# A state-space layer on one core: bias by matmul, a shorter softplus, a reordered instruction list and a split prologue

## The reference, cut to what matters

```
xz  = in_proj_w @ xn            # 512 rows: x half (256), z half (256)
for each direction (forward, reversed):
    u     = silu(conv4(x) + conv_bias)                     # 256 channels, 4 taps
    x_dbl = xproj_w @ u                                    # 8 rows for delta, 16 B, 16 C
    delta = softplus(dtproj_w @ x_dbl[:8] + dt_bias)
    dA    = exp(delta * A);  dBx = delta * B * u           # 256 channels x 16 states
    h[t]  = dA[t] * h[t-1] + dBx[t]                        # the scan
    y     = (sum over states of h * C + D * u) * silu(z)
branch 1 = out_proj_w @ (y_forward + y_reversed)
branch 2 = ternary(weight) @ quantize4(hadamard(xn))       # per-token scale, round, clip to -8..7
```

## Time and profile before

| | |
|---|---|
| median of three runs | 982.82 us |
| profiled execution | 989.38 us, span 987.6 us |
| TensorE busy | 802.9 us, 81% |
| VectorE busy | 787.0 us, 80% |
| ScalarE busy | 780.7 us, 79% |
| GpSimd busy | 788.1 us, 80% |
| mean granted clock of TensorE | 0.875 of 2.4 GHz |
| DMA, mean over the span | 73 GB/s |

### The profile page before, as it was taken

The page is one execution under the profiler, slowest core; times in us unless marked ns, Lnnn a source line. Parts: engine busy times, 40 slices in busy tenths (PEclk is TensorE's granted clock), DMA queues, the critical chain, the costliest instruction groups (busy, mean ns, idle before and its releaser), DMA issues.

```text
span 987.6 us, 13840 instructions
## 1 busy us (share of the span) xinstructions
PE 802.9 (81%) x3873; PEld 381.5 (39%) x3873; DVE 787.0 (80%) x795; ACT 780.7 (79%) x1452; POOL 788.1 (80%) x493
## 2 busy tenths in 40 slices
PE   2478887979888897888889797897978889797974
PEld 1134434343443434333353434434343343434352
DVE  2248887988888888888789887888978887988982
ACT  2469896988959887798869889698887988699950
POOL 1038978997899887898789977989879897798994
PEclk9677998899998989889879989889898898898796
DMA  3070607051160605215070421607043150704300
GB/s 86 11 162 29 135 4 182 3 123 41 57 136 3 159 3 124 68 53 107 3 170 24 115 44 39 154 3 159 3 104 88 33 129 3 169 15 99 61 22 11
DMA packets 50841, 72.44 MB, mean 73 GB/s; under 512 B 6128, under 2 KB 19328, under 8 KB 50816
## 3 DMA queue, kind: packets, MB, share of 16 engines
q1 hardware_dynamic: 50384, 71.87, 31.3%
q10 hardware_dynamic: 432, 0.26, 0.1%
HBM read 60.58 MB, written 11.53 MB: 73 GB/s over the span
## 4 chain that ended last, share of the span: by engine, by line
POOL 33%; issue 32%; ACT 13%; PE 11%; DVE 7%; SPq 1%; DMA 1%; POOLq 1%; DVEq 0%; ACTq 0%
POOL hst L612 22%; ACT da L370 5%; POOL dbx_t L622 5%; DVE hst L512 4%; PE pb L744 3%; ACT dbx_t L359 3%; POOL t_log L628 3%; PE b_ps L827 2%; PE b_ps L824 2%; POOL xn L674 2%; DVE b_ps L500 1%; PE pb L751 1%; PE y L841 1%; DMA rep<-d_scr 1%; PE pb L771 1%
## 5 line engine op out<-in xcount | busy, mean ns | idle before, releaser
L612 POOL TENSOR_TENSOR hst<-hst,c_rep 128x1024 f32<-128x1024 f32 x256 | 601.4, 2365 | 132.2 <-DVE hst L512 128.4
L512 DVE TENSOR_TENSOR_SCAN hst<-da,b_ps 128x512 f32<-128x512 f32 x512 | 589.5, 1203 | 82.1 <-ACT da L370 43.4
L827 PE MATMUL b_ps<-ident,dbx_t 128*128 128x128 f32 x1536 | 241.9, 298 | 127.3 <-DVE hst L512 120.1
L370 ACT ACTIVATE da<-rep,neg_a 128x511 f32<-128x511 f32 x512 | 335.6, 709 | 6.4 <-DMA rep<-d_scr 6.3
L827 PEld LDWEIGHTS b_ps<-ident,dbx_t 128*128 128x128 f32 x1536 | 178.2, 150 | 277.5 <-DVE hst L512 230.1
L359 ACT ACTIVATE dbx_t<-du_t,b_t 128x256 f32<-128x256 f32 x576 | 248.1, 495 | 2.9 <-PE b_ps L827 2.9
L841 PE MATMUL y<-hst,sum_sel 128*32 128x512 f32 x1024 | 166.6, 730 | 0.0
L744 PE MATMUL pb<-xnt,conv_wt 128*128 128x512 f32 x256 | 120.7, 616 | 0.7 <-ACT xnt L291 0.7
L824 PE MATMUL b_ps<-t_log,spread_sel 32*128 32x512 f32 x256 | 89.3, 698 | 10.6 <-DVE hst L512 10.6
L500 DVE TENSOR_TENSOR b_ps<-b_ps,b_rep 128x1024 f32<-128x1024 f32 x64 | 78.1, 1220 | 21.6 <-PE b_ps L824 21.6
L622 POOL TENSOR_TENSOR dbx_t<-du_t,b_t 128x1024 f32<-128x1024 f32 x48 | 91.2, 1901 | 2.7 <-ACT du_t L342 2.7
(11 more groups left out here) (90 smaller groups left out, 598.5 us busy)
## 6 DMA issues: line engine op xcount, KB each, us to landing
rep<-d_scr SPq DMA_DIRECT2D x128, 256.0 KB, 9.3
c_rep<-bc_scr SPq DMA_DIRECT2D x64, 256.0 KB, 5.0
d_scr<-t_pos SPq DMA_DIRECT2D x16, 512.0 KB, 3.0
b_rep<-bc_scr SPq DMA_DIRECT2D x64, 64.0 KB, 2.4
x_ln<-x SPq DMA_DIRECT2D x8, 256.0 KB, 3.2
x_res<-x SPq DMA_DIRECT2D x8, 256.0 KB, 2.9
out<-x_res SPq DMA_DIRECT2D x8, 256.0 KB, 9.5
conv_wt<-conv_w SPq DMA_DIRECT2D x2, 512.0 KB, 5.9
```

The costliest lines, as they stand in the source:

```text
L370: nc.scalar.activation(da[s % 2][:, j, 1:L], rep[d][h][:, j, 1:L], ACT.Exp, scale=neg_a[:, d, h, j, q:q + 1]).then_inc(decay_done, 1)
L512: nc.vector.tensor_tensor_scan(hst[s % RING][:, j, :], da[s % 2][:, j, :], b_ps[:, j, :], 0.0, ALU.mult, ALU.add).then_inc(scan_done, 1)
L612: nc.gpsimd.tensor_tensor(hst[s % RING][:, two, :], hst[s % RING][:, two, :], c_rep[d][:, q:q + 1, :].broadcast_to([P, 2, L]), ALU.mult).t ...
L827: ins = tr(b_ps[:, j, P * c:P * (c + 1)], dbx_t[(NX * d + q - 1) % 2][:, c, NJ * h + j, :, :].rearrange("p r e -> p (r e)"), ident[:, :])
```

## The change

Five things are done together.

Bias by matmul: row 64 of `dtw` holds the convolution's bias, and `conv` ends each half with a fifth matmul, that one row against a broadcast one. `u_sigmoid` is then one tanh pass; `make_u` is (tanh + 1) * `pb`, twice u, and factors of 0.5 and 0.25 go into `xproj` and `skip`. The bias of delta comes in the same way, through a row of `dtw` and a row of ones in `xdbl`.

Softplus: the Relu passes go; 1 + exp is written to `t_pos` in SBUF rather than to `pb`, `log1p` works on `t_pos`, and `delta` takes max(`pb`, 0) itself.

Lists: on ScalarE, VectorE (`times_b` one scan earlier), GpSimd and TensorE (both convolution halves in slot 7 of both units) the order is another one.

Quantizer: clip and rescale are VectorE's, in slot 6, on `pb`.

Prologue: ScalarE waits for the weights later, the two halves of the first unit's softplus, delta, du and replication go separately, and B and C are replicated first.

```diff
@@ TensorE
                 for k in taps:
-                    ins = mm(pb[:, 1 - h, :], conv_wt[d][:, k, P * h:P * (h + 1)], window, start=k == 0, stop=k == TAPS - 1)
+                    mm(pb[:, 1 - h, :], conv_wt[d][:, k, P * h:P * (h + 1)], window, start=k == 0, stop=False)
+                ins = mm(pb[:, 1 - h, :], dtw[d][BIAS:BIAS + 1, P * h:P * (h + 1)], ident[BIAS:BIAS + 1, BIAS:BIAS + 1].broadcast_to([1, L]), start=False, stop=True)
...
                     if s == 7 and not last(b):
                         if d == 0:
-                            conv(d, U + 2, 1, range(TAPS), dut_ready, 2 * V + 2)
-                        else:
-                            conv(d, U + 2, 0, range(TAPS), dut_ready, 2 * V + 1)
+                            pe.wait_ge(xnt_ready, b + 2)
+                        conv(d, U + 2, 0, range(TAPS), dut_ready, 2 * V + 1)
                     next_inputs(s, 1)
...
                     if s == 6 and nxt:
                         if d == 1:
-                            du_transposed(V, 1, had_read, b + 1)
-                        elif not last(b):
-                            pe.wait_ge(xnt_ready, b + 2)
-                            conv(d, U + 2, 0, range(TAPS), dut_ready, 2 * V + 1)
-                    if s == 7 and d == 1 and not last(b):
+                            du_transposed(V, 1, xq_ready, b + 1)
+                    if s == 7 and not last(b):
                         conv(d, U + 2, 1, range(TAPS), dut_ready, 2 * V + 2)
@@ ScalarE
-                nc.scalar.activation(t_exp[:, h, :], pb[:, 1 - h, :], ACT.Tanh, bias=half_bias[:, d, h:h + 1], scale=0.5).then_inc(u_step, 1)
-                act.wait_ge(u_step, 2 * V + h + 1)
-                nc.scalar.activation(t_exp[:, h, :], t_exp[:, h, :], ACT.Copy, bias=0.5, scale=0.5).then_inc(u_sig, 1)
+                nc.scalar.activation(t_exp[:, h, :], pb[:, 1 - h, :], ACT.Tanh, scale=0.5).then_inc(u_sig, 1)
...
-                nc.scalar.activation(xdbl[d][0:XC, :], pb[0:XC, 1, :], ACT.Copy).then_inc(xdbl_ready, 1)
+                nc.scalar.activation(xdbl[d][0:XC, :], pb[0:XC, 1, :], ACT.Identity, bias=ident[0:XC, ONE:ONE + 1]).then_inc(xdbl_ready, 1)
...
             def softplus_in(d, V):
+                for n, h in enumerate((1, 0)):
+                    act.wait_ge(dt_filled, 2 * V + n + 1)
+                    nc.scalar.activation(t_exp[:, h, :], pb[:, h, :], ACT.Abs).then_inc(sp_step, 1)
-                    nc.scalar.activation(t_exp[:, h, :], pb[:, h, :], ACT.Abs, bias=col[:, d, 1, h:h + 1]).then_inc(sp_step, 1)
-                    nc.scalar.activation(t_pos[:, h, :], pb[:, h, :], ACT.Relu, bias=col[:, d, 1, h:h + 1]).then_inc(sp_step, 1)
...
-                nc.scalar.activation(pb[:, :, :], t_exp[:, :, :], ACT.Copy, bias=1.0).then_inc(sp_step, 1)
+                nc.scalar.activation(t_pos[:, :, :], t_exp[:, :, :], ACT.Copy, bias=1.0).then_inc(sp_step, 1)
...
-                nc.scalar.activation(t_log[:, :, :], pb[:, :, :], ACT.Ln).then_inc(log_ready, 1)
+                nc.scalar.activation(t_log[:, :, :], t_pos[:, :, :], ACT.Ln).then_inc(log_ready, 1)
@@ ScalarE's list of a unit, after
+                for s in range(SLOTS):
+                    decays(b, d, s, 0)
+                    if s == 0:
+                        if d == 0 and not first(b):
+                            keep_dut(d, U, 1)
+                        inputs_t(d, U, 1, 1)
+                    if s == 1:
+                        inputs_t(d, U, 1, 3)
+                        if nxt:
+                            u_sigmoid(e, V, 1)
+                    if s == 2:
+                        if nxt:
+                            keep_xdbl(e, V)
+                        if d == 0 and not first(b):
+                            keep_xqt(b - 1)
+                        inputs_t(d, U, 2, 2)
+                    if s == 3 and nxt:
+                        softplus_log(V)
+                        if d == 0 and not last(b):
+                            log_var(b + 1)
+                    if s in (4, 5):
+                        inputs_t(d, U, 3, 2 * (s - 4))
+                    if s == 6 and d == 0 and not last(b):
+                        normalize(b + 1)
+                    if s == 7 and d == 0:
+                        if not last(b):
+                            keep_xnt(b + 1)
+                        keep_dut(e, V, 0)
+                    decays(b, d, s, 1)
+                    if s == 0:
+                        inputs_t(d, U, 1, 2)
+                        if nxt:
+                            u_sigmoid(e, V, 0)
+                    if s == 1:
+                        inputs_t(d, U, 2, 0)
+                        inputs_t(d, U, 2, 1)
+                    if s == 2:
+                        inputs_t(d, U, 2, 3)
+                        if nxt:
+                            keep_bt(e, V)
+                            softplus_in(e, V)
+                    if s == 3 and d == 0 and not last(b):
+                        guess_rstd(b + 1)
+                    if s in (4, 5):
+                        inputs_t(d, U, 3, 2 * (s - 4) + 1)
+                    if s == 5 and d == 0:
+                        z_sigmoid(b)
+                    if s == 6 and d == 0:
+                        keep_longer(b)
+                    if s == 7 and nxt:
+                        keep_dut(e, V, 1 - d)
+                        inputs_t(e, V, 1, 0)
@@ VectorE
-                nc.vector.scalar_tensor_tensor(u[d][:, h, :], pb[:, 1 - h, :], col[:, d, 0, h:h + 1], t_exp[:, h, :], ALU.add, ALU.mult).then_inc(u_ready, 1)
+                nc.vector.scalar_tensor_tensor(u[d][:, h, :], t_exp[:, h, :], 1.0, pb[:, 1 - h, :], ALU.add, ALU.mult).then_inc(u_ready, 1)
...
-                nc.vector.scalar_tensor_tensor(pb[:, :, :], pb[:, :, :], 1.0, t_log[:, :, :], ALU.subtract, ALU.subtract).then_inc(cor_step, 1)
+                nc.vector.scalar_tensor_tensor(t_pos[:, :, :], t_pos[:, :, :], 1.0, t_log[:, :, :], ALU.subtract, ALU.subtract).then_inc(cor_step, 1)
                 dve.wait_ge(cor_step, 2 * V + 1)
-                nc.vector.scalar_tensor_tensor(pb[:, :, :], pb[:, :, :], 0.0, t_exp[:, :, :], ALU.max, ALU.subtract).then_inc(cor_step, 1)
+                nc.vector.scalar_tensor_tensor(t_pos[:, :, :], t_pos[:, :, :], 0.0, t_exp[:, :, :], ALU.max, ALU.subtract).then_inc(cor_step, 1)
...
-                nc.vector.tensor_tensor(t_pos[:, :, :], t_pos[:, :, :], pb[:, :, :], ALU.subtract).then_inc(delta_ready, 1)
+                nc.vector.scalar_tensor_tensor(t_pos[:, :, :], pb[:, :, :], 0.0, t_pos[:, :, :], ALU.max, ALU.subtract).then_inc(delta_ready, 1)
...
                 for c in range(NC):
-                    ins = nc.vector.tensor_scalar(xq[:, c, :], pb[:, 0, P * c:P * (c + 1)], qinv[:, c:c + 1], ROUND, ALU.mult, ALU.add)
-                ins.then_inc(had_read, 1)
+                    at = slice(P * c, P * (c + 1))
+                    ins = nc.vector.tensor_scalar(pb[:, 0, at], pb[:, 0, at], qinv[:, c:c + 1], ROUND, ALU.mult, ALU.add)
+                ins.then_inc(xq_step, 1)
+                dve.wait_ge(xq_step, 2 * b + 1)
+                nc.vector.tensor_scalar(pb[:, 0, :], pb[:, 0, :], ROUND, Q_POS, ALU.subtract, ALU.min).then_inc(xq_step, 1)
+                dve.wait_ge(xq_step, 2 * b + 2)
+                for c in range(NC):
+                    ins = nc.vector.tensor_scalar(xq[:, c, :], pb[:, 0, P * c:P * (c + 1)], -Q_NEG, qscale[:, c:c + 1], ALU.max, ALU.mult)
+                ins.then_inc(xq_ready, 1)
...
                 for s in range(SLOTS):
+                    if s == 0:
+                        times_b(b, d, 0, 0)
                     scan(b, d, s, 0)
+                    if s < NH:
+                        times_b(b, d, s, 1)
                     if s == 0 and nxt:
                         make_u(e, V, 0)
...
                     scan(b, d, s, 1)
+                    if s < NH - 1:
+                        times_b(b, d, s + 1, 0)
                     if s == 0:
                         if nxt:
                             make_u(e, V, 1)
@@ SyncE, prologue
+            store_bc(0, 0)
+            load_bc(0, 0)
+            sp.wait_ge(first_delta, 1)
+            sp.dma_start(d_scr[0][0], t_pos[:, 0, :]).then_inc(first_stored, DMA)
+            sp.wait_ge(first_stored, DMA)
+            load_delta(0, 0)
+            sp.wait_ge(delta_ready, 1)
+            sp.dma_start(d_scr[0][1], t_pos[:, 1, :]).then_inc(delta_stored, DMA)
+            sp.wait_ge(delta_stored, DMA)
+            load_delta(0, 1)
```

220 lines of the change are left out of this document (112 added, 108 removed).

## The result

The changed kernel takes **1013.38 us** (four runs, 1011.82 to 1013.39), the kernel before 981.32 us beside it on the same chip (four runs, 978.13 to 986.75). The ratio is 1.0317, 95% interval 1.0267 to 1.0367: slower by 3.2%, where 955 us was forecast.

What follows compares the result with a forecast made beforehand. No single engine bounds the kernel: four are 84 to 86% busy and late hand-overs to VectorE's scans set the time. 989.4 - 12 (start) - 6 (end) - 10 (loop) = 961, over 1.0067 = 955 us; range 928 to 1004.

Steps and rivals of the forecast that it cites:

- step 2: VectorE's order: earlier B-multiply saves 1.0 us a batch, make_u 0.25; log1p and delta keep three passes of 1.22 us.
- step 4: TensorE: fifth matmul 0.86 us per convolution half; both halves in slot 7 make a 12.75 us burst, +4.6 us a batch.
- step 3: Quantizer: clip and rescale add 1.9 us a batch to VectorE; a new 2.0 us wait behind TensorE's late transposes.
- step 1: ScalarE: dropped passes and new list remove forward decay waits of 3.7 us a batch, another of 2.34, and 1.9 of logarithm wait.
- the last division: End of the sum: 961 us divided by 1.0067, from the profiled execution to the median, giving 955 us.
- rival A: log1p's SBUF operands make VectorE and GpSimd exclude each other in the loop: +35 to +53 us, 990 to 1008; chance 0.26.
- Step 5: Loop sum per batch: 9.8 us gone, 8.5 new, net -1.3, -10 us over 7.5 batches; bounds -34 and +30.
- step 6: Start: earlier normalize and first unit's work in halves bring the first scan to near 51.5 us; -12 us (-8 to -14).
- step 7: End: VectorE making xq in slot 6 lets the last sum and gating come earlier; -6 us (-4 to -6.5).
- Rival B: TensorE becomes the bound at the unit's edge, a cold stretch in its burst adding 3 us a batch: 978 us; chance 0.15.
- Rival C: ScalarE's relief is worth more, new waits replacing others in the loop: -35 us instead of -10, about 930 us; chance 0.10.

Runs made afterwards that it cites:

- experiment 1: Changed kernel with both log1p passes reading their first operand from PSUM (delta then differs from the reference's): 976.88 us, ratio 0.9963.
- experiment 2: Kernel before with 1 + exp written to a new SBUF buffer, so both log1p passes read two SBUF operands: 1016.7 us, ratio 1.0381.
- experiment 4: Changed kernel without the fifth matmul of each convolution half, so the convolution's bias is left out: 993.9 us, ratio 1.013.
- experiment 6: Changed kernel with VectorE's multiply with B directly before its scan again, after make_u and gate_y: 1001.82 us, ratio 1.0226.
- experiment 5: Changed kernel with the forward unit's convolution half 0 back in slot 6 and half 1 in the middle of slot 7: 1030.02 us, ratio 1.0508.
- experiment 9: Changed kernel with Relu passes and log1p in PSUM back, and the multiply with B directly before its scan: 967.38 us, ratio 0.9854.
- experiment 14: Kernel of experiment 9 with the convolution's bias as before: no fifth matmul, second ScalarE pass for the sigmoid, bias in make_u: 952.47 us, ratio 0.9729.
- experiment 13: Kernel of experiment 9 with the quantizer's clip and rescale back on GpSimd in all batches but the last: 967.44 us, ratio 0.9884.
- experiment 10: Kernel before with only the changed kernel's split prologue, adapted to the old softplus: 968.73 us, ratio 0.9866.
- experiment 11: Kernel before with the new prologue, and clip and rescale on VectorE in the last batch alone: 967.49 us, ratio 0.9883.
- experiment 12: Changed kernel with log1p's first operand from PSUM, no fifth matmul, and the multiply with B directly before its scan: 955.89 us, ratio 0.9735.
- experiment 15: Kernel of experiment 9 with both the quantizer back on GpSimd (but the last batch) and the bias as before: 951.21 us, ratio 0.9684.

## Why the prediction was wrong, step by step

VectorE's groups by line and its waits, both cut to the stretch from the first to the last scan, in us:

| | before | after | measured | predicted |
|---|---|---|---|---|
| log1p's two passes | 36.9 | 76.3 | +39.4 | 0 (step 2) |
| waits for the copies | 7.8 | 63.3 | +55.5 | +34.5 (step 4) |
| quantizer, with gaps | 9.3 | 24.6 | +15.3 | +14 (step 3) |
| waits for decays | 42.6 | 6.5 | -36.1 | -49.5 (step 1) |
| waits for the logarithm | 24.0 | 17.7 | -6.3 | -14 (step 1) |
| a scan's waits for TensorE | 29.0 | 13.6 | -15.4 | +15 (step 3) |
| gap after the B-multiply | 8.3 | 3.2 | -5.1 | -7.5 (step 2) |
| make_u | 22.0 | 20.3 | -1.7 | -1.9 (step 2) |
| the rest (scans -4.9, others) | | | -2.2 | 0 |
| sum | | | +43.4 | -9.4 |

The sum of the rows is the +42.3 us of the timeline to 1.1.

**The step that failed is step 2**, in the words "log1p and delta keep three passes of 1.22 us": delta's pass is 1.19, and log1p's are 2.10 and 2.99. The forecast was 58 us off. 39.4 of it is this step, 12 are all other rows of the loop together, and 6 come from the last division: the execution behind the profile of before stood 0.67% above its median, the changed kernel's did not. Experiments 1 and 2 show that the operands' place alone does it, in both kernels, by about 36 us.

So it is rival A, and in its mechanism as well as in its price: "the second waits one product", and where GpSimd was first the first pass waits too. In the loop all 15 second passes wait for a product to end and 15 first passes for the rest of one, +2.6 us a unit, 39.4 us within its 35 to 53. Its total, 990 to 1008, lies under the measured 1013 because of the 12 us of the other rows and the 6 of the division. I had no row on the pair and took the duration of another pairing, delta's with an operand in PSUM, for it. A 26% chance on a mechanism that the Trainium skill, "SBUF — State Buffer", section "Who interferes with whom", states for exactly this pair, against nothing but a missing row, was too little; the trace agrees with that page, 2.81 us where the product beside takes 1.90 alone and 3.26 where it takes 2.37.

**Step 4** had the mechanism and too small a size: 4.2 us of copy waits per unit (63.3 / 15), taken at 2.8. The burst was 13.4 us long, forecast at 12.75, and VectorE had some 9.5 us of work beside it instead of 10.0. The fifth matmul was priced rightly at 0.86 us and is worth 19.5 us (experiment 4). That VectorE's order makes it worse was said there without a price; it is 11.6 us (experiment 6). That the convolutions' place in slot 7 was a cost was false with the lists as they are: back in slot 6 the kernel loses 17 us (experiment 5).

**Step 1** was roughly right where it counted: the decay waits went, by three quarters of what I gave. But the passes saved are not the reason: with the Relu passes back, and with the second tanh pass back too, the decay waits are still gone (7.1 us in experiment 9, 8.0 in 14, 5.1 of each at the start). As to time, the Relu passes are about 2 us (experiment 9, if the gains of 1 and 6 add), and with the second tanh pass back in place of the matmul the kernel is 15 us faster (14). What is left as the reason is the order of the lists, ScalarE's first of all; no run changed that alone, so it is argued, not shown. Step 5's upper end has a slip: half of ScalarE's 8.5 us would give +3 a batch, +22 us, not +30.

**Step 3**: VectorE's 1.9 us a batch were there, 15.3 us; the new 2.0 us wait on TensorE did not show in VectorE's row, where a scan's waits for TensorE fell by 15.4. In the kernel of experiment 9 the quantizer's two places are worth the same (experiment 13).

**Steps 6 and 7** were right in their sums: -12.2 us where -12 was given, -6.1 where -6 was. Both hold in the kernel before too (10.2 in the profile of experiment 10, 6.1 in that of 11). In step 6 some luck is in it: the first convolution starts at 16.04 us, not near 14.2, since ScalarE waits 3.34 us for GpSimd before it can normalize, and half 0's delta is there at 41.31, not 40.5; the first scan, at 51.6, is where it was forecast all the same.

Rival B's burst is there, but at full clock (the granted clock from 468.1 to 481.5 is 1.00, and its convolutions take 3.70 us, as before), and its price is that of step 4. Rival C did not come: even with the prices off (experiments 9, 12, 15) the time is 951 to 967 us, and more than half of what the fastest gains on the kernel before is steps 6 and 7: 14.1 us at the start and 6.1 at the end, of 38.1 between the two profiled executions.

## What to carry to other kernels

Ask of every operand that a change moves from PSUM to SBUF which other engine reads SBUF at that moment; a VectorE pass with two SBUF operands waited for GpSimd's product under way to end, 1.3 us more a pass here, and the profile shows that as a longer pass, not as a wait. A kernel that has no such pass has no row of it, and an average over passes hides it: look at the single durations. A pass taken off an engine is worth the wait that ends at it, and here ScalarE waited 71.5 us for the convolution at the place where its pass was saved, while the matmul that replaced it lay on the path. Causes that stand behind one burst do not add: three edits worth 67.6 us one by one were worth 57.5 together.
